# Expert tiles in fours instead of pairs, with single buffers between the steps

## The chip, the cores and the metric

The kernel runs on one core of a Trainium2 chip. The metric is the time of one execution on the device in microseconds (us), lower is better. The kernel before took 1149.71 us, the median of 3 runs (1145.74 to 1151.64).

## The reference

Two transformer layers over 2048 tokens of width 128. Layer 0 has full attention with 16 heads of 8, layer 1 causal attention with 8 heads of 16. Between them stands the part that the change touches, a mixture of 16 experts of which each token takes one, beside a shared network:

```python
logits = hidden @ router_w.T
top_vals, top_idx = jax.lax.top_k(logits, 1)
scores = sigmoid(top value at its expert, 0 elsewhere)
gate, up = split(einsum('nth,nhf->ntf', hidden * scores, gate_up_proj))
routed_out = einsum('ntf,nfh->nth', up * silu(gate), down_proj)
shared = silu(hidden @ shared_gate_w.T) * (hidden @ shared_up_w.T) @ shared_down_w.T
x = x + gb * (shared + routed_out.sum(axis=0))
```

Layer 1 then normalises x again, projects keys, queries and values, and ends with a token-mixing network of its own.

## The kernel before

The tokens are worked on in four chunks of 512. A planner written in Python (make_plan) puts all the work of the kernel into one list of named stages. Each engine's program walks through this list and emits its own part of each stage, so the order within every engine is that of the list. The backbone is 336 steps of attention (256 for layer 0, 80 for layer 1). A step has two pairs of transposed scores ("st", L846 in layer 0, L855 in layer 1), which ScalarE turns into exponentials (L1351), score tiles for the row maxima ("s", L805 and L812), which VectorE reduces (L1120), and the product of probabilities and values ("pv", L875).

All other work is booked into a step with at(), at_side(). TensorE's stages wait in a book called later, and do_later() takes one of them, that of the earliest step, at each call. There are two calls in a step (three from the last unit of layer 0 on). A second book, after, holds the work of layer 1's mixing network and is served when nothing in the first is due. at_side() is for stages without TensorE, done when their step comes.

A tensor of results in PSUM takes a turn of a bank. There are three single banks T0 to T2, taken in rotation by beside() and by the transposed scores, and two double banks S0 and S1, taken in turn by between() and the score tiles. A turn waits until the engine that empties the bank has freed it.

The tokens of chunks 0 to 2 (group 0, 28 tiles of 128) and of chunk 3 (group 1, 20 tiles) are sorted by expert: GpSimd scatters them to memory, SyncE loads them back (XS). The tiles go through three products, now by pairs:

- m0: two tiles are transposed into one T bank (L951), ScalarE copies them to hS (L1407).
- m1: gate and up products of both tiles into one bank of an S turn (L961). ScalarE takes tanh of the gates into tS (L1413), VectorE multiplies twice (L1237, L1241) into acS and frees the bank.
- m2: the down products into a T bank (L969), ScalarE copies them back to XS (L1417), and SyncE stores every second pair's four tiles (L1699).

hS, tS and acS have two buffers each. The weights of an expert tile are one fetch of 192 KB by SyncE (L1693) into one of 16 slots in group 0 and 8 in group 1; a slot is fetched anew when the m2 of its earlier tile is done on TensorE.

When a group is through, GpSimd gathers the results (L1590), and setup1 prepares a chunk for layer 1 at fixed steps: acceptance and statistics on VectorE (L1247, L1249, L1070, L1074), the turn (L764), the projections k1 and q1 (L776), whose parts VectorE splits (L1092 to L1096), SyncE stores and loads again (L1631, L1653, L1660), and the values (L791), which VectorE copies (L1254). Layer 1 may compute score tiles of a chunk from three steps after its projections on. The shared network runs beside as four "up" stages (L919, L920, with L1401, L1180, L1184) and a "down" (L929, freed by L1189).

Of the kernel before, what the change touches and what calls it, by code (L numbers as in the profile page):

```python
# [13 lines left out]
CH = 512  # L14
# [93 lines left out]
def make_plan():  # L108
# [23 lines left out]
    def at_side(step, *fns):  # L132
        at(step, *fns, book=light)
# [57 lines left out]
    def experts(s, g, pace):  # L191
        n = GROUPS[g][3] // 2

        def first(p):
            if p < n:
                beside("m0", g, p)
            if 0 <= p - 2 < n:
                beside("m2", g, p - 2)
                for k in (2 * p - 4 + SLOTS[g], 2 * p - 3 + SLOTS[g]):
                    if k < GROUPS[g][3]:  # L200
                        P.stage("fetch", g, k)
        for p in range(n + 2):
            at(s + int(pace * p), lambda p=p: first(p))
            if 0 <= p - 1 < n:
                at(s + int(pace * p), lambda p=p: between("m1", g, p - 1))
        return s + int(pace * (n + 1)) + 1
# [6 lines left out]
    def setup1(s, c):  # L213

        def accept():
            P.stage("accept", c)
            P.stage("stats", 2, c)

        def turn():
            P.turn_h(2, c, P.next_t())  # L220
            P.xb += 1
            P.stage("bias1", c)

        def rows():
# [5 lines left out]
            ready[c] = now[0] + 3  # L230

# [19 lines left out]
    def after_chunk(L, c, t):  # L251
# [5 lines left out]
        elif c == 2:  # L257
# [4 lines left out]
            s = experts(s, 0, 1)  # L262
            for i in range(3):
                at_side(s, lambda i=i: P.stage("gather", i))
            shared(s - 1, 1, 1)
            setup1(s + 3, 0)
            setup1(s + 5, 1)
            shared(s + 4, 2, 1)
            setup1(s + 9, 2)
        else:  # L270
# [3 lines left out]
            s = experts(s, 1, 0.6)  # L274
            at_side(s, lambda: P.stage("gather", 3))
            setup1(s + 3, 3)
# [221 lines left out]
def adaln_two_layers(nc, A, out):  # L498
# [3 lines left out]
    with ctx:  # L502
# [100 lines left out]
        hS, tS, acS = ([Vf[:, 6656 + 512 * k + 256 * i:6656 + 512 * k + 256 * i + 256] for i in range(2)] for k in range(3))  # L603
# [95 lines left out]
        def gates_ups(bank):  # L699

            v = bank.rearrange("p (k two n) -> p k two n", k=2, two=2)
            return v[:, :, 0, :], v[:, :, 1, :]

        def two_before(g, p):

            return (g, p - 2) if p >= 2 else (0, GROUPS[0][3] // 2 - 2 + p) if g else None
# [1053 lines left out]
```

## Time and profile before

| | |
|---|---|
| median of 3 runs | 1149.71 us |
| profiled execution, its own time | 1151.61 us |
| its span, first to last instruction | 1149.2 us |
| TensorE busy | 1021.7 us, 89% |
| VectorE busy | 903.9 us, 79% |
| ScalarE busy | 814.9 us, 71% |
| GpSimd busy | 149.0 us, 13% |
| mean granted clock of TensorE | 0.949 |

Busy time is the share of the span in which an engine executes instructions. An engine that is busy for most of a stretch sets its length; where none is, the waits between them do. So the table by stretch and the waits within a stretch tell more than the whole. The granted clock is the share of full TensorE speed, where 1 stands for 2.4 GHz and 0.5 for 1.2 GHz. Expert products of group 0 run from about 645 to 713 us, those of group 1 from about 890 to 943 us.

### The profile page before, as it was taken

The numbers are of one execution on the slowest core, as the hardware profiler recorded it, in microseconds if no ns is written. First come the engines' busy times: TensorE is split into PE (matmuls) and PEld (weight loads), VectorE is DVE, ScalarE is ACT, GpSimd is POOL, SyncE is SP. The second block draws the span as 40 slices with busy tenths as digits, with TensorE's granted clock in tenths as the row PEclk, the third lists the DMA queues.
The fourth block names the chain that finished last, engine by engine and source line by source line (L and its number), as shares of the span: only waits on it lengthen the run. The fifth ranks groups of instructions, "written<-read, shape, count | busy, mean of one in ns | idle before, by whom it ended". The sixth has DMA issues, their size and how long they took to land.

```text
span 1149.2 us, 22131 instructions
## 1 busy us (share of the span) xinstructions
PE 1021.7 (89%) x8766; PEld 349.2 (30%) x8766; DVE 903.9 (79%) x1154; ACT 814.9 (71%) x1556; POOL 149.0 (13%) x264
## 2 busy tenths in 40 slices
PE   4658999999999999999998999899978888798895
PEld 1212222222222222222232444343434443233323
DVE  5897999998999989999988777666766568587602
ACT  3105999998999998999976676567743555466683
POOL 2005000004000013000034000410121003000100
PEclk8658999999999999999999999999989999899997
DMA  4650400002000001000003431052003211200000
GB/s 105 128 98 17 137 2 2 2 2 44 1 2 2 2 21 23 2 1 3 2 2 116 122 87 31 27 93 49 1 1 111 74 57 28 38 10 2 10 1 9
DMA packets 47259, 42.04 MB, mean 37 GB/s; under 512 B 6102, under 2 KB 45366, under 8 KB 47158
## 3 DMA queue, kind: packets, MB, share of 16 engines
q1 hardware_dynamic: 44902, 35.27, 13.2%
q0 software_dynamic: 1824, 5.25, 1.6%
q8 instruction: 70, 1.15, 0.4%
q14 instruction: 31, 0.25, 0.1%
q10 hardware_dynamic: 432, 0.13, 0.0%
HBM read 26.83 MB, written 13.30 MB: 35 GB/s over the span
## 4 chain that ended last, share of the span: by engine, by line
PE 65%; DVE 21%; ACT 7%; issue 3%; DMA 2%; POOL 1%; SPq 1%; POOLq 0%; DVEq 0%; ACTq 0%
PE O L875 23%; DVE mx L1120 13%; PE T L846 12%; PE S L805 7%; PE S L812 4%; ACT PT L1351 3%; PE T L855 3%; PE S L961 2%; PE S L919 1%; PE S L929 1%; PE T L969 1%; PE S L920 1%; PE S L855 1%; PE T L884 1%; DVE Vf L1180 1%
## 5 line engine op out<-in xcount | busy, mean ns | idle before, releaser
L1120 DVE TENSOR_REDUCE mx<-S 128x2 f32<-128x1024 f32 (+2 forms) x672 | 757.0, 1179 | 89.2 <-PE S L812 38.2
L1351 ACT ACTIVATE PT<-T 128x512 f32<-128x512 f32 (+2 forms) x1280 | 675.8, 581 | 118.1 <-PE T L846 46.8
L875 PE MATMUL O<-PT,Va 128*9 128x256 f32 (+1 forms) x4040 | 319.0, 388 | 3.3 <-ACT Os L1358 3.3
L805 PE MATMUL S<-Ks,Qs 48*128 48x512 bf16 x1024 | 208.0, 397 | 26.3 <-DVE mx L1120 22.0
L846 PE MATMUL T<-Qs,Ks 51*128 51x512 bf16 x1024 | 202.1, 387 | 15.3 <-ACT PT L1351 7.2
L846 PEld LDWEIGHTS T<-Qs,Ks 51*128 51x128 bf16 x1024 | 55.6, 93 | 226.4 <-issue 131.9
L875 PEld LDWEIGHTS O<-PT,Va 128*9 128x9 f32 x4040 | 60.0, 88 | 207.4 <-issue 198.0
L812 PE MATMUL S<-K,Qs 96*128 96x512 bf16 (+3 forms) x320 | 85.5, 358 | 15.7 <-DMA Qs<-rows_q 5.4
L855 PE MATMUL T<-Qs,K 99*128 99x512 bf16 (+3 forms) x256 | 72.2, 350 | 7.7 <-ACT PT L1351 4.0
L875 PE MATMUL O<-PT,V 128*17 128x512 f32 (+3 forms) x640 | 75.0, 541 | 0.0
L805 PEld LDWEIGHTS S<-Ks,Qs 48*128 48x128 bf16 x1024 | 52.5, 95 | 53.4 <-DVE mx L1120 47.9
L1530 POOL CAST n<-nm 128x16 bf16<-128x16 f32 x24 | 5.6, 233 | 411.8 <-DVE nm L1128 411.6
L1336 ACT ACTIVATE nrow<-T 12x512 bf16<-12x512 bf16 x24 | 14.1, 586 | 47.2 <-PE T L825 47.1
L812 PEld LDWEIGHTS S<-K,Qs 96*128 96x128 bf16 x320 | 29.2, 99 | 53.1 <-issue 13.7
L855 PEld LDWEIGHTS T<-Qs,K 99*128 99x128 bf16 x256 | 22.7, 99 | 45.3 <-issue 33.3
L1139 DVE RECIPROCAL rl<-T 128x16 f32<-128x16 f32 x8 | 2.0, 254 | 42.8 <-PE T L884 42.8
L1180 DVE SCALAR_TENSOR_TENSOR Vf<-Vf,S 128x512 f32<-128x512 f32 x16 | 11.0, 687 | 30.6 <-ACT Vf L1401 30.5
L1345 ACT ACTIVATE PT<-S 128x1024 f32<-128x1024 f32 (+3 forms) x32 | 28.5, 941 | 7.0 <-PE S L855 5.6
L1237 DVE SCALAR_TENSOR_TENSOR Vf<-Vf,S 128x256 f32<-128x256 f32 x24 | 10.1, 421 | 28.2 <-ACT Vf L1413 28.2
L1401 ACT ACTIVATE Vf<-S 128x512 f32<-128x512 f32 x16 | 9.6, 597 | 31.1 <-PE S L920 31.1
L1309 ACT ACTIVATE hT<-T,mc 128x512 f32<-128x512 f32 x16 | 12.5, 779 | 26.4 <-PE T L764 26.1
L1545 POOL TENSOR_TENSOR vw<-om,rl 128x128 f32<-128x128 f32 x16 | 6.5, 407 | 185.6 <-DVE rl L1134 185.6
(225 smaller groups left out, 835.3 us busy)
## 6 DMA issues: line engine op xcount, KB each, us to landing
Qs<-in_L_ffn_experts SPq DMA_DIRECT2D x28, 192.0 KB, 2.7
Ks<-in_L_ffn_experts SPq DMA_DIRECT2D x20, 192.0 KB, 2.6
Qs<-rows_q SPq DMA_DIRECT2D x48, 64.0 KB
Vf<-sorted_x SPq DMA_DIRECT2D x12, 256.0 KB, 4.5
sorted_y<-Vf SPq DMA_DIRECT2D x12, 256.0 KB, 2.3
Qs<-rows_q SPq DMA_DIRECT2D x24, 128.0 KB, 4.6
rows_q<-q SPq DMA_DIRECT2D x7, 384.0 KB, 2.6
sorted_x<-XP POOLq DMA_DIRECT2D x1, 1792.0 KB, 10.8
```

Of the source, the lines that this page charges most:

```text
L805: m = e.matmul(two[:, i, :], Qs[r0:r0 + 48, hp, q0:q0 + 128], Ks[r0:r0 + 48, hp, CH * kb:CH * kb + CH], start=True, stop=True, tile_positi ...
L812: m = e.matmul(two[:, i, 0:n], Q1[0:96, 4 * quad + 2 * pair + i, q0:q0 + 128], K1[0:96, CH * kb:CH * kb + n], start=True, stop=True)
L846: m = e.matmul(bank, Ks[r0:r0 + 51, hp, keys], Qs[r0:r0 + 51, hp, CH * c:CH * c + CH], start=True, stop=True, tile_position=(r0, 0))
L855: m = e.matmul(bank[:, lo:CH], K1[0:99, keys], Q1[0:99, 4 * quad + 2 * pair + i, CH * c + lo:CH * c + CH], start=True, stop=True)
L875: m = e.matmul(Ob[32 * g:32 * g + d1, lo:hi], v, PT[(2 * j + g // 2) % 4][:, p0 + lo:p0 + hi], start=(kt == 0 and halves[0] == 0), stop=Tr ...
L961: m = e.matmul(bank[:, 256 * k + 128 * h:256 * k + 128 * h + 128], w_of(g, i)[:, 128 * h:128 * h + 128], hS[p % 2][:, 128 * k:128 * k + 12 ...
L1120: e.tensor_reduce(mx[:, u % 2, h0:h0 + 2, kb], two[:, :, 0:n], AX.X, ALU.max).then_inc(free, 1)
L1180: dv.tick(e.scalar_tensor_tensor(bt, bsg, 1.0, two[:, 0, :], ALU.add, ALU.mult))
L1309: e.activation(hc(c), bank, ACT.Identity, bias=mc[:, layer, k:k + 1], scale=mc[:, layer, k + 1:k + 2]).then_inc(free, 1)
L1336: e.activation(nrow[:, U % 2, :], bank.bitcast(BF16)[0:12, 0:CH], ACT.Copy).then_inc(free, 1)
L1345: e.activation(both, Sb[turn["st", L, j, 2 * pair][0]][:, :, lo:CH], ACT.Exp).then_inc(free, 1)
L1351: e.activation(PT[(2 * j + pair) % 4][:, CH * i + lo:CH * i + CH], bank[:, lo:CH], ACT.Exp).then_inc(free, 1)
```

## The change

Tiles go through the three products by fours. m0 fills a whole T bank with four turned tiles. m1 takes both banks of an S turn, four gates in the first and four ups in the second, so that tanh and the multiplications are of 512 columns. m2 fills a whole T bank with four results, and each m2 is followed by its store and the fetches into its four slots. hS, tS and acS have one buffer of 512 columns each in the same memory. The planner books m1 of a four and m0 of the next into one step, and m2 into the step after; fours are 2 steps apart in group 0 and 1.2 in group 1.

What comes after the experts is no longer booked at fixed steps: the last m2 calls then(), which books gathers and setup1, and each part of setup1 books the next when it has been staged. Acceptance is put off while the shared "down" of its chunk is not yet planned.

```diff
+    def experts(s, g, pace, then):
+        n = GROUPS[g][3] // 4
+        def last(q):
+            beside("m2", g, q)
+            for k in range(4 * q + SLOTS[g], min(4 * q + 4 + SLOTS[g], GROUPS[g][3])):
+                P.stage("fetch", g, k)
+            if q == n - 1:
+                then(now[0] + 1)
+        at(s, lambda: beside("m0", g, 0))
+        for q in range(n):
+            t = s + 1 + int(pace * q)
+            at(t, lambda q=q: between("m1", g, q))
+            if q + 1 < n:
+                at(t, lambda q=q: beside("m0", g, q + 1))
+            at(t + 1, lambda q=q: last(q))
+        return s + 1 + int(pace * (n - 1)) + 2
...
         def accept():
+            if ("down", c) not in P.turn:
+                at_side(now[0] + 1, accept)
+                return
             P.stage("accept", c)
             P.stage("stats", 2, c)
+            at_side(now[0] + 1, lambda: P.norm(2, c))
+            at(now[0] + 2, turn)
...
-        at_side(s + 1, lambda: P.norm(2, c))
-        at(s + 2, turn)
-        at(s + 3, rows)
-        at(s + 4, values)
...
-            s = experts(s, 0, 1)
+            def rows1(s):
+                for i in range(3):
+                    at_side(s, lambda i=i: P.stage("gather", i))
+                setup1(s + 3, 0)
+                setup1(s + 5, 1)
+                shared(s + 4, 2, 1)
+                setup1(s + 9, 2)
+            s = experts(s, 0, 2, rows1)
...
-            s = experts(s, 1, 0.6)
+            experts(s, 1, 1.2, rows1)
...
-        hS, tS, acS = ([Vf[:, 6656 + 512 * k + 256 * i:6656 + 512 * k + 256 * i + 256] for i in range(2)] for k in range(3))
+        hS, tS, acS = (Vf[:, 6656 + CH * k:6656 + CH * k + CH] for k in range(3))
...
+                    two = Sb[turn["m1", g, q][0]]
+                    done(("m0", g, q))
+                    for k in range(4):
+                        i = 4 * q + k
                         pe.wait_ge(w_fetched[g][i % SLOTS[g]], 16 * (i // SLOTS[g] + 1))
                         for h in range(2):
+                            m = e.matmul(two[:, h, 128 * k:128 * k + 128], w_of(g, i)[:, 128 * h:128 * h + 128], hS[:, 128 * k:128 * k + 128],
+                                         start=True, stop=True)
...
-                    e.activation(two_tiles(tS[p % 2]), gates_ups(bank)[0], ACT.Tanh, scale=0.5).then_inc(expert_sig, 1)
+                    e.activation(tS, bank, ACT.Tanh, scale=0.5).then_inc(expert_sig, 1)
```

## Rows read from the trace of the kernel before

**Rows 1.** Busy time by stretch (us from the span's start)

```profile
core 0: us, PE busy (x) PEld busy (x) DVE busy (x) ACT busy (x) POOL busy (x), PEclk, DMA share, GB/s
644.50:713.75 69.25, 66.65 (x605) 32.15 (x601) 51.17 (x64) 51.52 (x112) 1.27 (x5) 1.00 0.21 59
...
889.80:943.40 53.60, 43.58 (x320) 26.15 (x319) 30.86 (x44) 26.72 (x66) 0.87 (x4) 1.00 0.22 64
943.40:969.30 25.90, 23.29 (x149) 10.62 (x146) 22.75 (x38) 15.54 (x29) 8.01 (x11) 1.00 0.08 22
```

**Rows 2.** Waits of TensorE, 890 to 945 us: total, times, longest

```profile
PE T L969 <- DVE Vf L1241: 3.8, 6, 1.0
PE S L961 <- DVE mx L1120: 2.3, 3, 0.9
PE S L812 <- DVE Vf L1241: 1.7, 3, 0.7
```

**Rows 3.** Timeline of TensorE in group 0: start, length, instruction

```profile
672.54 1.16 PE L961 MATMUL S<-Vf,Qs 128*128 128x128 f32 x8
673.63 0.39 PE L846 MATMUL T<-Qs,Ks 51*128 51x512 bf16 x2
673.85 0.38 PE L805 MATMUL S<-Ks,Qs 48*128 48x512 bf16 x2
...
674.71 0.44 PE L951 MATMUL T<-idf,Vf 128*128 128x128 f32 x2
675.24 0.68 PE L969 MATMUL T<-Qs,Vf 128*128 128x128 f32 x4
675.86 0.39 PE L846 MATMUL T<-Qs,Ks 51*128 51x512 bf16 x2
...
687.94 0.66 PE L884 MATMUL T<-idf,Os 128*128 128x128 f32 x4
688.52 0.39 PE L846 MATMUL T<-Qs,Ks 51*128 51x512 bf16 x2
```

**Rows 4.** Groups of instructions by shape: count, busy us, mean ns, idle before

```profile
L1120 DVE TENSOR_REDUCE mx<-S 128x2 f32<-128x1024 f32 x624 | 725.3, 1217 | 74.8 <-PE S L812 38.2 <-PE S L805 26.2 <-PE S L815 8.3
...
L1180 DVE SCALAR_TENSOR_TENSOR Vf<-Vf,S 128x512 f32<-128x512 f32 x16 | 11.0, 687 | 30.6 <-ACT Vf L1401 30.5
...
L1237 DVE SCALAR_TENSOR_TENSOR Vf<-Vf,S 128x256 f32<-128x256 f32 x24 | 10.1, 421 | 28.2 <-ACT Vf L1413 28.2
...
L1401 ACT ACTIVATE Vf<-S 128x512 f32<-128x512 f32 x16 | 9.6, 597 | 31.1 <-PE S L920 31.1
...
L1413 ACT ACTIVATE Vf<-S 128x256 f32<-128x256 f32 x24 | 9.2, 383 | 24.0 <-PE S L961 23.9
```

**Rows 5.** Timeline of TensorE, single places; idle time and its end in brackets

```profile
754.00 0.65 PE L764 MATMUL T<-idf,XP 128*128 128x128 f32 x4 [1.20 <-DVE V L1254]
...
902.89 1.16 PE L961 MATMUL S<-Vf,Ks 128*128 128x128 f32 x8
...
905.51 0.60 PE L812 MATMUL S<-K,Qs 96*128 96x512 bf16 x2 [0.59 <-DVE Vf L1241]
...
969.29 1.02 PE L776 MATMUL T<-hT,wk 128*16 128x512 f32 x2
...
987.24 1.87 PE L812 MATMUL S<-K,Qs 96*128 96x512 bf16 x4 [5.40 <-DMA Qs<-rows_q]
```

**Rows 6.** Timeline of VectorE: acceptance of chunk 1, split of chunk 3

```profile
742.69 0.68 DVE L1247 TENSOR_TENSOR XP<-XP,gB 128x512 f32<-128x512 f32 x1
...
745.04 0.38 DVE L1074 BATCH_NORM_AGGREGATE mv<-st 128x2 f32<-128x6 f32 x4
...
971.63 0.68 DVE L1092 TENSOR_TENSOR qf<-qf,q 16x512 f32<-16x512 f32 x1 [1.19 <-ACT q L1325]
...
974.57 0.69 DVE L1096 TENSOR_TENSOR q<-qf,q 128x512 bf16<-128x512 f32 x1
```

**Rows 7.** Timeline of SyncE's queue: two fetches of group 1

```profile
897.13 1.13 SPq L1693 DMA_DIRECT2D Ks<-in_L_ffn_experts  x2
```

**Rows 8.** The page's DMA issues: fetches of group 1, us to landing

```profile
Ks<-in_L_ffn_experts SPq DMA_DIRECT2D x20, 192.0 KB, 2.6
```

More of the change, by code:

```diff
@@ L189, in sort @@
         return s + 2
[L191 to L206, printed above, removed]
+    def experts(s, g, pace, then):
[14 more added lines that the diff above has]
+        return s + 1 + int(pace * (n - 1)) + 2
     def shared(s, c, apart):
@@ L222, in turn @@
             P.stage("bias1", c)
+            at(now[0] + 1, rows)
         def rows():
@@ L230, in rows @@
             ready[c] = now[0] + 3
+            at(now[0] + 1, values)
         def values():
@@ L273, in after_chunk, with rows1 @@
             shared(t + 6, 3, 1)
-            s = experts(s, 1, 0.6)
-            at_side(s, lambda: P.stage("gather", 3))
-            setup1(s + 3, 3)
+            def rows1(s):
+                at_side(s, lambda: P.stage("gather", 3))
+                setup1(s + 3, 3)
+            experts(s, 1, 1.2, rows1)
     P.stage("silu")
@@ L697, in w_of, with four_before @@
             return Wt[g][k % SLOTS[g]]
[L699 to L706, printed above, removed]
-        def two_tiles(v):
-            return v.rearrange("p (k n) -> p k n", k=2)
+        def four_before(g, q):
+            return (g, q - 1) if q else (0, GROUPS[0][3] // 4 - 1) if g else None
         def pe_program(e):
@@ L946, in pe_program @@
                 elif name == "m0":
-                    g, p = a
-                    bank, full = opened(("m0", g, p))
-                    pe.wait_ge(x_sorted[g][p // 2], 16)
-                    for k in range(2):
-                        m = e.transpose(bank[:, 128 * k:128 * k + 128], XS[:, 2 * p + k, :], idf[:, :])
+                    g, q = a
+                    bank, full = opened(("m0", g, q))
+                    pe.wait_ge(x_sorted[g][q], 16)
+                    for k in range(4):
+                        m = e.transpose(bank[:, 128 * k:128 * k + 128], XS[:, 4 * q + k, :], idf[:, :])
@@ L952, in pe_program @@
                     m.then_inc(full, 1)
                 elif name == "m1":
-                    g, p = a
-                    bank, full = opened(("m1", g, p))
-                    done(("m0", g, p))
-                    for k in range(2):
-                        i = 2 * p + k
+                    g, q = a
+                    _, full = opened(("m1", g, q))
+                    two = Sb[turn["m1", g, q][0]]
+                    done(("m0", g, q))
+                    for k in range(4):
+                        i = 4 * q + k
@@ L963, in pe_program @@
                     m.then_inc(full, 1)
                 elif name == "m2":
-                    g, p = a
-                    bank, full = opened(("m2", g, p))
-                    done(("m1", g, p))
-                    for k in range(2):
-                        m = e.matmul(bank[:, 128 * k:128 * k + 128], acS[p % 2][:, 128 * k:128 * k + 128], w_of(g, 2 * p + k)[:, 256:384],
-                                     start=True, stop=True)
+                    g, q = a
+                    bank, full = opened(("m2", g, q))
@@ L971, in pe_program @@
+                    done(("m1", g, q))
+                    for k in range(4):
+                        m = e.matmul(bank[:, 128 * k:128 * k + 128], acS[:, 128 * k:128 * k + 128], w_of(g, 4 * q + k)[:, 256:384], start=True, stop=True)
                     m.then_inc(full, 1)
```

61 lines of the change are left out of this document (25 added, 36 removed).

## Prediction

> **What bounds the kernel now.** I read the table of busy time by stretch first. In the first expert stage (group 0, 644.5 to 713.75 us) TensorE is busy 66.65 of 69.25 us, VectorE 51.17 and ScalarE 51.52 [rows 1]. So every instruction that TensorE issues there costs, and the other two have cover. In the second (group 1, 889.8 to 943.4) TensorE is busy 43.58 of 53.6 us, and no other engine more than 30.86 [rows 1]: here waits set the pace. Behind it (943.4 to 969.3) VectorE is busy 22.75 of 25.9 us [rows 1].
>
> The chain of waits of group 1 names them: products m2 that wait for VectorE's activation (3.8 us, 6 times), products m1 that wait for a score reduction to empty their bank (2.3 us, 3 times), and score tiles that wait until m1's bank is empty (1.7 us, 3 times) [rows 2]. Together 7.8 us; smaller ones bring the idle time of the stretch to 10.0 us.
>
> **The change, part by part.**
>
> *TensorE's work.* Products and transposes are the same in number; only the turns halve, 72 to 36. In the timeline of group 0 the eight records of m1 take 1.09 us to the next instruction, the four of m2 0.62 [rows 3]. The slope is 0.1175 us a record, so 0.15 us of each turn is fixed; joining two saves 0.15 for m1 and for m2. Two transposes take 0.53 us to the next instruction, four (those of the attention result) 0.58 [rows 3]: joining saves 0.48. Per four tiles 0.78 us; seven fours in group 0 give 5.5 us. In group 1 I take 0.6 each, since fixed parts there lie partly under waits: 3.0 us.
>
> *The chain through ScalarE and VectorE.* It becomes longer for each turn. Half-width instructions took 383 ns (tanh), 421 and about 421; full-width ones of the same kind 597, 687 and about 687 [rows 4]. The bank of m1 comes free at 905.51 behind an m1 of 902.89 [rows 5]; less its 1.09 that is 1.5 us, of which 1.2 are the three instructions and 0.3 hand-over. After the change it is 2.0 + 0.3 = 2.3 us. ScalarE and VectorE save some 36 fixed parts of 0.17 us and a few of 0.15; both have cover, so I count nothing for it.
>
> *New stall, group 0.* Each step of layer 0 has two score tiles, and there are two banks. Now m1 and the next tile of its bank are far enough apart. After the change the plan puts m1 ahead of the first pair of transposed scores, and the next m0 in the second slot. Between m1 and the second score tile, on m1's bank, lie: first half of the step 1.08 us [rows 3], m0 of four 0.58, the second pair 0.22 (673.63 to 673.85). That is 1.88 us against 2.3: a stall of 0.4, six times, and 0.95 at the last four, which has no m0 to fill it. ScalarE's queue is tighter too (a 0.6 us copy and tanh ahead of the exponentials): 0.15 more for each four. New stalls 0.4 x 6 + 0.95 + 0.15 x 7 = 4.4 us. They take most of the 5.5. Gain in group 0: about 1 us (bounds: 5.5 if the stalls stay hidden, -3 if ScalarE's delays double them).
>
> *Group 1.* Pace 1.2 and three slots a step: m1 comes behind the two score tiles, so each of four m1 waits about 0.9 for the reduction of its bank (a reduction takes 1217 ns [rows 4]; the products of the other tile, 0.60 us by their record [rows 5], of which I count 0.43 before the next can start, cover part, and hand-over adds 0.1). The first m1 has its bank's next tile 0.86 behind it: 1.4 us. Three m2 follow at 1.9 us a chain of 2.3: 0.4 each. Sum 1.4 + 3.6 + 1.2 = 6.2, against 10.0 idle now: 3.8 gained, of which I leave 0.8 for waits that I don't see. With the 3.0 of turns it is 6.0 us. The planner's queue also empties sooner: the last m2 is staged at step 279, not 280; the mixing turn of chunk 0 moves from 281 to 278 and its products from 283 and 285 to 280 and 282. That work is not lost, but leaves the stretch where VectorE is nearly full [rows 1], which is why I let the 6.0 us pass through. Bounds 2 and 9.
>
> *Setup of layer 1.* setup1 now chains itself. By hand through the planner's queues: gathers at step 232 (before 233), acceptance of chunk 0 at 235 (236), but its projections k1, q1 at 240 (239), since the shared products of chunk 2 hold slots ahead of it. In step 240 come projections of chunk 0, the shared result of 32 records (at the slope above 3.8 us), and projections of chunk 1; before, the two chunks' projections were two steps apart. Scores of layer 1 start at 243 (242). Queued on VectorE behind one another are then: split of chunk 0, result of chunk 2, split of chunk 1, acceptance and statistics of chunk 2, and only then the copy of chunk 0's values, which frees the T bank that the values of chunk 1 want (they are three T turns apart). Prices: the split begins 2.3 us after the projection (969.29 to 971.63) and both parts take 3.6 (to 975.26); acceptance with statistics takes 2.7 us (742.69 to 745.42) [rows 5, 6]. From the first projection: the second ones start at 2.0 + 0.3 + 3.8 + 0.3 = 6.4 (two projections, a pair of transposed scores, the shared result, a pair), their split at 8.7, its end at 12.3, acceptance 15.0, copy 15.2. TensorE comes to chunk 1's values at 6.4 + 2.0 + 1.0 + 1.0 + 0.3 = 10.7 (projections, probabilities, chunk 0's values, a pair; eight records of the slope are 1.0). A stall of some 4.5 us; the kernel now pays 1.20 us at the like place (754.00 [rows 5]). Net loss 3.3, with other small waits 3.5 us (bounds 0, if the copy comes earlier than I think, and 6). It covers the loads of q1, which need 18 us from projection to landing (969.29 to 987.24 [rows 5]): TensorE would be at the first score after about 21.
>
> *Unchanged.* The wait of 5.40 us for q1 of chunk 3 at 987.24 [rows 5]: gather, acceptance and projection stay at steps 280, 283, 286, scores at 289. The loads start from the projection, so the wait moves with it, whole. Stores stay 12, fetches 48. Group 1 has only eight weight slots: the four fetches behind one m2 must land before the next m1 but one, about 9.2 us later. One takes 2.6 us to land [rows 8], they leave SP some 0.8 us apart (two starts within 1.13 less 0.33 [rows 7]), and the copy and the store ahead of them take about 1.7: first landed after 4.7, fourth after 7.1, and it is wanted 1.5 later than the first. Hidden, with 3 us to spare.
>
> **Sum.** -1 - 6 + 3.5 = -3.5 us. The profiled execution has a span of 1149.2 and its own time is 1151.61, the median 1149.71: the gain carries over as it is, since all of it lies inside. Forecast 1149.7 - 3.5 = 1146.2, rounded to 1146.
>
> **A rule against the change.** The rows show what grows: m1's bank is held 0.8 us longer a turn [rows 4]. The Trainium skill, page "Perfetto Trace Analysis", section "Optimizing Scalar/DVE Operations", says that where ScalarE and VectorE are not saturated but cause bubbles on other engines, breaking instructions up may let work complete sooner; this change does the reverse. By it the time would be that of the third rival below; the trace agrees in part, for bubbles exist in group 1 and hardly in group 0.
>
> **Rivals.**
> - *No new stall in setup.* The values' copy is in time; the rest as above. 1149.7 - 7.0 = 1142.7. For it: now 1.20 us suffices; against it: the queue worked out above. Chance 0.24.
> - *The gain is taken back.* Group 1 gains only its turns (3.0), group 0 nothing, setup loses as said: 1150. Chance 0.14.
> - *Long chains bind in both stages.* Each four pays at its bank (2.3 less 1.1) and at m2 (0.6): 1.8 us a four, 21.6 for twelve, against 8.5 of turns and 7.8 of present waits saved; with setup 21.6 - 16.3 + 3.5 = 8.8 slower, 1158.5. It decides from (16.3 - 3.5) / 12 = 1.07 us a four on. For it: single buffers and two banks; against it: m0 lies between m1 and the bank's next use. Chance 0.11.
> - *Weights late in group 1.* If SP stands behind ScalarE's copies 3 us longer, three m1 wait 3 us each: +9 - 3.5, 1155. The slack of 3 us would have to go. Chance 0.05.
> - *The forecast* 0.46, own range 1142.5 to 1149.5.
>
> **Numbers.** A change of 0.5% (5.75 us) is about what a measurement of this kernel can tell from none: below 1144.0 is faster, above 1155.5 slower. Faster: the first rival, less a little, and a quarter of the forecast's own range, 0.34. Slower: most of the third and a part of the weights, 0.13. Same 0.53. The range 1140 to 1156 leaves out the upper half of the chains' rival and the case in which no new stall comes and group 1 gains its full 9.
>
> **What would show it.** Group 0: idle time of TensorE for VectorE at a score tile of 0.4 us, once each four, and m1 of 16 records in about 2.05 us to the next instruction. Group 1: its expert products over some 4 to 6 us sooner after their start, m2's waits at most three. Setup: one wait of TensorE of 3 to 5 us for VectorE's copy of the values, ahead of the second products of values, around 40 us behind the last expert product of group 0. If that wait is absent the first rival holds; if the wait of 5.40 has changed by more than 1 us, my reading of the q1 chain is wrong. A granted clock that falls behind the new stall, as at 987.24, where four score products took 1.87 us, would cost up to 1.5 us more.

## The result and the profile after

| | before | after |
|---|---|---|
| median of 16 runs each | 1149.85 us | 1155.39 us |
| lowest and highest | 1145.37 to 1153.24 | 1151.67 to 1157.06 |
| profiled execution, own time | 1151.61 us | 1152.05 us |
| its span | 1149.2 us | 1150.0 us |

The changed kernel is slower: ratio 1.0049, 95% interval 1.0036 to 1.0061, some 5.6 us. The profiled execution of before was one of its slow ones and that of after one of its fast ones, so these two profiles differ by 0.4 us only. They show where the kernel changed, not the whole of the loss.

The busy time by stretch, the same stretches as before [rows 1]:

```profile
core 0: us, PE busy (x) PEld busy (x) DVE busy (x) ACT busy (x) POOL busy (x), PEclk, DMA share, GB/s
644.50:713.75 69.25, 65.63 (x584) 32.82 (x576) 47.61 (x49) 45.45 (x88) 4.63 (x9) 1.00 0.22 65
889.80:943.40 53.60, 46.12 (x342) 27.82 (x340) 31.53 (x37) 28.24 (x59) 3.46 (x7) 1.00 0.25 71
943.40:969.30 25.90, 22.70 (x130) 9.61 (x130) 22.16 (x38) 12.25 (x23) 6.60 (x9) 0.93 0.06 17
```

TensorE works 46.12 us in the second stretch where it worked 43.58. The waits there, from 890 to 945 us (total, times, longest), stand against [rows 2]:

```profile
PE S L963 <- DVE mx L1121: 3.4, 4, 0.9
PE S L813 <- DVE Vf L1241: 1.3, 1, 1.3
PE T L971 <- DVE Vf L1241: 1.2, 3, 0.4
PE S L813 <- DVE mx L1121: 1.1, 3, 0.5
PE T L885 <- ACT Vf L1407: 0.3, 1, 0.3
PE T L971 <- ACT nrow L1336: 0.2, 1, 0.2
```

In the changed file m0 is L952, m1 L963, m2 L971, a transposed score pair L847 in layer 0, a score tile L806 in layer 0 and L813 in layer 1. Group 0 in TensorE's timeline, against [rows 3]:

```profile
665.09 2.05 PE L963 MATMUL S<-Vf,Qs 128*128 128x128 f32 x16
667.07 0.39 PE L847 MATMUL T<-Qs,Ks 51*128 51x512 bf16 x2
...
668.16 0.66 PE L952 MATMUL T<-idf,Vf 128*128 128x128 f32 x4
668.90 0.39 PE L847 MATMUL T<-Qs,Ks 51*128 51x512 bf16 x2
669.34 0.39 PE L806 MATMUL S<-Ks,Qs 48*128 48x512 bf16 x2
...
672.64 0.39 PE L847 MATMUL T<-Qs,Ks 51*128 51x512 bf16 x2 [0.18 <-ACT PT L1351]
673.73 2.05 PE L963 MATMUL S<-Vf,Qs 128*128 128x128 f32 x16
...
704.24 0.39 PE L806 MATMUL S<-Ks,Qs 48*128 48x512 bf16 x2 [0.64 <-DVE Vf L1241]
```

One m1 of four takes 1.98 us to the next instruction (665.09 to 667.07), two of before took 2.18. The idle times in brackets are small: 0.18 for a probability tile once a four, and 0.64 at the last four. From one m1 to the next (665.09 to 673.73) a four takes 8.64 us, where two pairs took 8.81.

The setup of layer 1, in TensorE's timeline:

```profile
757.81 0.59 PE L777 MATMUL T<-hT,wk 128*16 128x512 f32 x1
758.33 1.13 PE L777 MATMUL T<-hT,wq 128*128 128x512 f32 x2
759.39 1.04 PE L876 MATMUL O<-PT,Va 128*9 128x512 f32 x8
760.36 1.06 PE L792 MATMUL T<-wv,hT 128*128 128x16 f32 x8
761.36 0.39 PE L847 MATMUL T<-Qs,Ks 51*128 51x512 bf16 x2
766.45 1.89 PE L792 MATMUL T<-wv,hT 128*128 128x16 f32 x8 [4.70 <-DVE V L1254]
768.27 0.61 PE L847 MATMUL T<-Qs,Ks 51*128 51x512 bf16 x2
```

This is the forecast stall: the second products of values wait 4.70 us for VectorE's copy of the first, where the kernel before waited 1.20 us for such a copy at 754.00 [rows 5]. What VectorE does in that time:

```profile
760.00 0.68 DVE L1093 TENSOR_TENSOR qf<-qf,q 16x512 f32<-16x512 f32 x1 [2.17 <-ACT q L1325]
...
762.95 0.69 DVE L1097 TENSOR_TENSOR q<-qf,q 128x512 bf16<-128x512 f32 x1
763.55 0.69 DVE L1247 TENSOR_TENSOR XP<-XP,gB 128x512 f32<-128x512 f32 x1
...
765.90 0.38 DVE L1075 BATCH_NORM_AGGREGATE mv<-st 128x2 f32<-128x6 f32 x4
766.20 0.19 DVE L1254 COPY V<-T 128x64 f32<-128x64 f32 x1
```

The split of chunk 1, then the acceptance and statistics of chunk 2, then the copy of 0.19 us for which TensorE stands. From 1 us into the wait on, the granted clock is at its lower level, 1.2 GHz, for most of 14 us:

```profile
757.00:763.00 6.00, 4.75 (x26) 1.69 (x24) 3.54 (x7) 4.98 (x9) 0.00 (x0) 0.98 0.44 130
763.00:777.00 14.00, 9.78 (x44) 4.11 (x44) 4.79 (x18) 3.97 (x8) 2.05 (x4) 0.52 0.80 131
```

So the waits that the prediction named in group 1 and in the setup are there; of the 0.4 us that it expected at a score tile in each four of group 0, only that of the last four is. What it did not foresee is that the sum has the other sign.

### The profile page after: what moved, and what is told of

It is laid out like the page before. It is cut to its first block, busy times and chain, and to the rows that moved or that the text cites. A ratio compares the mean times of both kernels' runs of the same rounds, so it can differ in the third digit from the quotient of the medians.

```text
span 1150.0 us, 21977 instructions
## 1 busy us (share of the span) xinstructions
PE 1021.5 (89%) x8758; PEld 351.4 (31%) x8758; DVE 900.5 (78%) x1130; ACT 807.6 (70%) x1520; POOL 148.9 (13%) x264
## 4 chain that ended last, share of the span: by engine, by line
PE 65%; DVE 20%; ACT 7%; issue 3%; DMA 2%; POOL 1%; SPq 1%; POOLq 0%; DVEq 0%; ACTq 0%
PE O L876 23%; DVE mx L1121 12%; PE T L847 12%; PE S L806 7%; PE S L813 4%; ACT PT L1351 3%; PE T L856 3%; PE S L963 2%; PE S L920 1%; PE S L921 1%; PE T L885 1%; PE T L971 1%; PE S L856 1%; PE S L930 1%; ACT PT L1345 1%
## 5 line engine op out<-in xcount | busy, mean ns | idle before, releaser
L876 PE MATMUL O<-PT,Va 128*9 128x256 f32 (+1 forms) x4032 | 319.8, 389 | 3.3 <-ACT Os L1358 3.3
L806 PE MATMUL S<-Ks,Qs 48*128 48x512 bf16 x1024 | 208.2, 398 | 28.6 <-DVE mx L1121 22.7
L847 PE MATMUL T<-Qs,Ks 51*128 51x512 bf16 x1024 | 203.1, 389 | 17.3 <-ACT PT L1351 10.2
L847 PEld LDWEIGHTS T<-Qs,Ks 51*128 51x128 bf16 x1024 | 55.9, 93 | 231.7 <-issue 131.2
L876 PEld LDWEIGHTS O<-PT,Va 128*9 128x9 f32 x4032 | 60.0, 89 | 204.2 <-issue 194.9
L813 PE MATMUL S<-K,Qs 96*128 96x512 bf16 (+3 forms) x320 | 86.0, 360 | 16.8 <-DVE mx L1121 6.3
L876 PE MATMUL O<-PT,V 128*17 128x512 f32 (+3 forms) x640 | 75.2, 543 | 0.0
L806 PEld LDWEIGHTS S<-Ks,Qs 48*128 48x128 bf16 x1024 | 52.7, 96 | 58.9 <-DVE mx L1121 48.3
L813 PEld LDWEIGHTS S<-K,Qs 96*128 96x128 bf16 x320 | 29.7, 99 | 54.9 <-issue 14.1
L816 PE MATMUL S<-mq,idb 128*128 128x128 bf16 x128 | 26.1, 223 | 0.0
```

Of the source, the lines that this page charges most:

```text
L806: m = e.matmul(two[:, i, :], Qs[r0:r0 + 48, hp, q0:q0 + 128], Ks[r0:r0 + 48, hp, CH * kb:CH * kb + CH], start=True, stop=True, tile_positi ...
L813: m = e.matmul(two[:, i, 0:n], Q1[0:96, 4 * quad + 2 * pair + i, q0:q0 + 128], K1[0:96, CH * kb:CH * kb + n], start=True, stop=True)
L816: m = e.matmul(two[:, i, n - 128:n], idb[:, :], mq[:, :], start=False, stop=True, skip_group_check=True)
L847: m = e.matmul(bank, Ks[r0:r0 + 51, hp, keys], Qs[r0:r0 + 51, hp, CH * c:CH * c + CH], start=True, stop=True, tile_position=(r0, 0))
L876: m = e.matmul(Ob[32 * g:32 * g + d1, lo:hi], v, PT[(2 * j + g // 2) % 4][:, p0 + lo:p0 + hi], start=(kt == 0 and halves[0] == 0), stop=Tr ...
```

## The experiments

Times are compared with runs of the kernel before on the same chip (its medians there 1158.1 to 1158.6 us). To tell where time went I measured, in each profile, the time between the same steps of the plan, each from the start of its first product of probabilities and values (L876 here). With it goes the time that the granted clock was at its lower level in that stretch, from the clock records of the same trace.

| kernel | setup of layer 1 | waits filled | ratio to before | 95% interval |
|---|---|---|---|---|
| changed kernel again | chained | no | 1.0033 | 1.0007 to 1.0059 |
| fours, fixed setup | fixed | no | 0.9997 | 0.998 to 1.0013 |
| pairs, chained setup | chained | no | 1.0062 | 1.0033 to 1.009 |
| fours, third chunk later | chained, +1 | no | 1.0022 | 1.0005 to 1.0039 |
| fours, second and third later | chained, +1 +1 | no | 1.0004 | 0.9981 to 1.0027 |
| fours in group 1 only | fixed | no | 1.0007 | 0.9987 to 1.0027 |
| the same, m1 in the third slot | fixed | no | 1.0020 | 1.0001 to 1.0039 |
| changed, one wait filled | chained | values' copy | 1.0040 | 1.0027 to 1.0052 |
| before, waits filled | fixed | the others | 0.9969 | 0.9955 to 0.9983 |
| fours, fixed setup, filled | fixed | the others | 0.9917 | 0.9899 to 0.9934 |
| changed, filled | chained | all | 0.9969 | 0.9956 to 0.9982 |
| changed, values first, filled | chained | the others | 0.9982 | 0.9969 to 0.9996 |
| fours in group 1 only, filled | fixed | the others | 0.9943 | 0.9931 to 0.9956 |
| fours in group 0 only, filled | fixed | the others | 0.9964 | 0.9946 to 0.9982 |

**First: is it the fours or the setup?** Theory setup puts the loss on the chained setup stages, theory chains on the longer single-buffered turns of four. The changed kernel with the setup stages at their fixed steps of before:

```diff
-                then(now[0] + 1)
+                then(now[0] + (1 if g else 2))
...
-            if ("down", c) not in P.turn:
-                at_side(now[0] + 1, accept)
-                return
...
+        at_side(s + 1, lambda: P.norm(2, c))
+        at(s + 2, turn)
+        at(s + 3, rows)
+        at(s + 4, values)
```

> The tiles stay in fours, but each part of the setup for layer 1 is booked at fixed steps again, as in the kernel before (projections of the chunks at steps 239, 241, 245 and scores from 242 on). Theory setup: the loss comes from TensorE's wait of 4.70 us for the copy of the values and from the half clock behind it; it goes away, and the time is about 1149 us, no more than the kernel before. Theory chains: the longer chains of single buffers cost in the expert stages; the time stays at about 1155 us.

Measured 0.9997. The pairs of before with the chained setup stages (the same chaining lines added to the kernel before):

```diff
         def accept():
+            if ("down", c) not in P.turn:
+                at_side(now[0] + 1, accept)
+                return
...
+            at_side(now[0] + 1, lambda: P.norm(2, c))
+            at(now[0] + 2, turn)
...
-        at_side(s + 1, lambda: P.norm(2, c))
-        at(s + 2, turn)
-        at(s + 3, rows)
-        at(s + 4, values)
```

> The kernel before with its pairs, but with the setup for layer 1 that books each of its parts when the one ahead is staged. Here the projections fall on steps 239, 241 and 245, so they do not meet in one step, and the values of chunk 1 come in step 242 behind the acceptance of chunk 2. Theory setup: a wait of 1 to 3 us for the values' copy, 1150 to 1152 us. Theory chains: the setup costs nothing, 1150 us.

Measured 1.0062. This is not the converse of the experiment ahead of it: with pairs the two chunks' projections fall on steps 239 and 241 as before, so chaining only changes the order within steps 240 and 241. And its executions fall into two groups, five at 1159.2 to 1162.2 us and seven at 1169.3 to 1172.1, with the profiled one among the long ones (the median of the kernel before is 1158.24 there). In that profile the wait for the values' copy is 0.7 us only, and steps 236 to 246 took 51.95 us, against 47.07 in the kernel before. The clock was at its lower level for 10.2 us of them, against 3.4, which can be up to 3.4 us of the difference. The rest, and why seven of twelve executions are 10 us longer, is open. That the loss of the changed kernel goes with its setup rests on the first experiment, and more firmly on the same pair of kernels with the waits filled (below): here the two intervals, 0.9997 and 1.0033, still touch.

The changed kernel once more, unchanged, on that chip:

> The changed kernel once more, for a second profile. Both theories: 1155 us; the profile shows how much of the time between the layers is the same in each execution: the wait of 4.7 us is there again, the stretches at half clock may lie elsewhere.

Measured 1.0033, which agrees with 1.0049. And the changed kernel with only the setup of the third chunk a step later, then with those of the second and the third:

```diff
-                setup1(s + 9, 2)
+                setup1(s + 10, 2)
```

> The changed kernel with the acceptance of chunk 2 one step later (242 for 241), so that VectorE copies the values of chunks 0 and 1 ahead of its 2.7 us. Theory setup: the wait of 4.70 us falls to about 2 us, and the half clock behind it may go; 1151 to 1153 us. Theory chains: no change from 1155 us.

Measured 1.0022; the wait for the values' copy is 1.79 us. Steps 236 to 246 took 45.5 us in its profile, less than in the kernel before (47.07), so what this variant still loses lies elsewhere: 1.1 us in steps 246 to 263, since the scores of layer 1 start at step 243 and not 242, and 2.0 in steps 292 to 305, with 6.8 us at the lower clock (below).

```diff
-                setup1(s + 5, 1)
+                setup1(s + 6, 1)
...
-                setup1(s + 9, 2)
+                setup1(s + 10, 2)
```

> The changed kernel with two setup stages of the next layer moved: the second chunk's one step later (its projection lands in the step after that of the first, 240 becomes 239 and 241), the third's one step later; the fours of both groups stay as they are. Theory setup (the 0.5% lies in the values' copy queued behind the splits and the acceptance, TensorE's wait of 4.70 us for it, and the half clock behind the wait): the wait for the first chunk's values' copy is under 2 us, no half-clock stretch of 13.7 us stands at 763 to 777, and the ratio to the kernel before is 0.998 to 1.001. Theory chains (fours with single buffers are what is lost): nothing is given back, ratio 1.003 to 1.006. A third reading, that any later chunk costs because its scores then start later (as the variant with only the third chunk moved gave 1.0022): 1.001 to 1.003.

Measured 1.0004. The wait is gone (1.06 us of products of values without idle time before them), and steps 236 to 246 took 46.51 us where the changed kernel took 49.49 on its second chip. The scores of layer 1 start at step 242 again (51.9 us for steps 246 to 263, not 53.0). By the ratios, the further the two chunks are pulled apart, the less is lost; the intervals of neighbours overlap.

**Second: where is the gain of the fours?** The fixed setup gives back the loss, but leaves no gain, though steps 263 to 292, with group 1, took 161.0 us in the fours with fixed setup and 165.3 in the kernel before. So I tried group 1 alone. The generator of the stage takes four or two tiles by group; the pair functions are those of the kernel before:

```diff
+W = (2, 4)
...
+            s = experts2(s, 0, 1)
```

> Pairs in group 0 as before, fours in group 1 alone, and the setup stages at their steps of before. Theory setup: group 1 alone gives about 2 us (steps 263 to 292 were 4.4 us shorter at their start and 2.4 us longer at their end), so the ratio is 0.996 to 0.999, under that of the fours in both groups with the old setup (0.9997), if group 0's fours cost anything at all in the scatter and gather stretches. Theory chains: group 1's chain of acceptance, gate copy and result waits costs more than the pairs', ratio 1.000 to 1.003.

Measured 1.0007, while its profile has steps 263 to 292 at 158.8 us, 6.5 us below the kernel before. Not all of that is the fours': 2.9 us of it lie ahead of group 1's first turned tiles, where this profile has 3.4 us at the lower clock and that of the kernel before 10.2. From those first turned tiles on the profiles sort by tiles and by clock:

| profile | tiles in group 1 | at the lower clock, us | first m0 of group 1 to step 292, us |
|---|---|---|---|
| before, both chips | pairs | 6.8 | 116.7 and 116.5 |
| before, waits filled | pairs | 3.4 | 116.6 |
| fours in group 0 only, filled | pairs | 0 | 115.0 |
| changed, first profile | fours | 13.7 | 116.7 |
| fours, fixed setup | fours | 10.2 | 115.1 |
| changed again; group 1 only | fours | 6.8 | 112.9 and 112.8 |
| fours, fixed setup, filled | fours | 3.4 | 113.1 |

Group 1's products themselves always gain the same: from the first m0 to the start of the last m2 it is 44.7 us in all eleven profiles with fours at this pace, and 52.7 in four of the five with pairs (54.3 in the pairs with chained setup). Of these 8.0 us, 4.3 are paid back before step 292. Of those, 2.9 are one new wait, of a score tile for a reduction on VectorE, which all eleven have and none of the five. At 6.8 us of lower clock 3.7 us are left. And in seven of the eleven the clock falls during that wait or within 2 us behind it, for 3.4 or 6.8 us, where no profile with pairs has it fall; in the changed kernel's first profile, with 13.7 us at the lower clock, nothing is left. There:

```profile
955.74 0.34 PE L813 MATMUL S<-K,Qs 96*128 96x384 bf16 x1 [2.85 <-DVE mx L1121]
...
958.98 1.91 PE L813 MATMUL S<-K,Qs 96*128 96x512 bf16 x4
```

Four such products take 1.03 us at the full clock (below). The same kernel with m1 a half step later, behind the second pair of transposed scores, and fours one step apart instead of 1.2:

```diff
-            at(t, lambda q=q: between("m1", g, q))
+            if q + 1 < n:
+                third[t] = lambda q=q: between("m1", g, q + 1)
```

> As the kernel with fours in group 1 alone, with the gates and ups of each four put into the step's third slot, a half step later than the turned tiles, so that TensorE has two score tiles between the turn and its copy's reader. If the waits of 0.8 to 0.9 us per four for the turned tiles' copy behind the score acceptance are worth their time, the waits at the gates and ups fall under 0.3 us each and the ratio is 0.994 to 0.998. If the stretch is held by VectorE (25.0 of 29.4 us busy in steps 280 to 286), the waits go and the time does not: 0.998 to 1.000. Theory chains: removing the waits gives back the loss, ratio 0.003 under that of fours in group 1 alone.

Measured 1.0020. The waits of m1 (L1001 here) for reductions are 0.3 us at most, as expected, but others took their place. Waits of TensorE from 890 to 960 us:

```profile
PE S L1001 <- DMA Ks<-in_L_ffn_experts: 5.1, 3, 3.1
PE S L848 <- DVE mx L1160: 1.1, 2, 0.9
PE T L891 <- ACT PT L1395: 0.9, 1, 0.9
PE S L1001 <- DVE mx L1160: 0.6, 2, 0.3
```

The weights are late: with fours one step apart there are fewer steps between a four's fetches and their use. That is the mechanism of the prediction's rival of late weights, and at pace 1.2 it has not come. Slot and pace were changed together, so the later slot by itself was not tried.

The kernel before was profiled on that chip too.

> The kernel before, for a profile on the same chip as the variants. If the stops of TensorE, ScalarE and VectorE during the scatters and gathers (about 4 us in steps 105 to 216 and 7 us in steps 231 to 236 in four profiles of variants) belong to the chip and not to the change, they stand here too.

1159.2 us, span 1157.4. The stops during the gathers stand here as well (ScalarE, then TensorE; see the last section), so they are not the change's.

Timeline of TensorE at the start of score unit 6 of layer 1, where it waits for the rows of shifts; first the kernel before:

```profile
1048.21 0.59 PE L855 MATMUL T<-Qs,K 99*128 99x512 bf16 x2 [2.48 <-DMA Qs<-nrow]
1048.64 1.03 PE L812 MATMUL S<-K,Qs 96*128 96x512 bf16 x4
```

Then the changed kernel, run again:

```profile
1046.87 1.01 PE L856 MATMUL T<-Qs,K 99*128 99x512 bf16 x2 [2.48 <-DMA Qs<-nrow]
1047.68 1.91 PE L813 MATMUL S<-K,Qs 96*128 96x512 bf16 x4
```

The same wait of 2.48 us, and behind it the same four score products take 1.03 us in one and 1.91 in the other. The table of stretches gives the granted clock there (1044 to 1058 us) as 1.00 and 0.76. Whether this wait is followed by the lower clock differed from profile to profile; steps 292 to 305 took 40.8 us with it absent and 42.1 to 43.1 with it present (absent in 5 profiles of the 11 in which the wait is unfilled). The mean granted clock of the timed runs says how much lower clock there is in all: 0.9513 (35 runs) and 0.9530 (29 runs) for the kernel before, and 0.9455 to 0.9496 for the seven variants above. At two levels, the time at the lower one is 2 x (1 - clock) x span: 109 to 113 us in the kernel before, 117 to 126 in the variants, the pairs with chained setup (0.9472) among them.

**Third: take the lower clock away.** TensorE executes added fp32 products with an unused result, in the bank that the next instruction has taken anyway, just ahead of its long waits. The work of the reference is as before.

```diff
+            def warm(bank, n):
+                if n:
+                    pe.wait_ge(po_const, PO["id"])
+                    for _ in range(n):
+                        e.matmul(bank[:, 0:128], idf[:, :], idf[:, :], start=True, stop=True)
...
+                        if c == 3 and rows_loaded["q1", c].name not in pe.met:
+                            warm(two[:, 0, :], 14)
...
+                    warm(bank0, {(0, 15, 1): 14, (1, 6, 0): 8, (1, 7, 0): 8}.get((L, u, kt), 0) if pair == 0 else 0)
```

The entry (0, 15, 1) is the place ahead of the values' copy; 14 more stand ahead of the last turned tile, 8 ahead of group 1's rank, 7 ahead of mix_k of the last chunk. First only the values' copy in the changed kernel:

> The changed kernel with 14 added fp32 products of 128 by 128 (results unused, some 3.4 us in all at the full clock) on TensorE just ahead of the transposed scores that stand before its wait of 4.70 us for the copied values, so that the wait is filled and the clock does not fall, while VectorE's queue is as late as before. Theory clock (the setup's cost is mostly the half clock behind the wait): the granted clock is 1.0 where it was half from 763 to 777, and the ratio is 0.002 to 0.004 under that of the changed kernel (1.0033 and 1.0049). Theory stall (the cost is the wait itself): the wait shrinks to about 1 us, the step ends as late as before, and the ratio stays at 1.003 to 1.005.

```profile
772.21 3.37 PE L727 MATMUL T<-idf 128*128 128x128 f32 x28
...
777.09 1.07 PE L798 MATMUL T<-wv,hT 128*128 128x16 f32 x8 [1.19 <-DVE V L1261]
```

The wait is filled (1.19 us left) and the products behind it run at the full clock (1.07 us, not 1.89), but the ratio is 1.0040, as without. The granted clock tells why this doesn't decide between the two theories:

```profile
765.00:779.00 14.00, 12.81 (x98) 8.85 (x96) 10.39 (x27) 6.64 (x13) 1.26 (x2) 1.00 0.65 127
779.00:786.00 7.00, 6.22 (x31) 1.99 (x24) 0.77 (x4) 3.58 (x8) 0.88 (x2) 0.51 0.63 110
```

The lower clock was put off, from right behind the wait to 2 us later, and not avoided. It shows as well that the wait costs by itself: with the clock full up to 779, steps 238 to 240 took 17.39 us, only some 1.4 less than without the products (18.72 and 18.86).

Then all the waits, in three kernels on the same chip:

> The kernel before with the same products ahead of the same waits, but for the values' copy, which waits for 1.2 us only. Theory clock: half-clock stretches of 6.8 us at the last chunk's queries and at the shift rows go, the ratio is 0.990 to 0.997. Theory stall: 0.999 to 1.002.

> Fours in both groups with the setup stages at their steps of before, and the same products as in the kernel before. If group 1's gain (3 to 6 us in the profiles of steps 263 to 292) is what the half clock behind the later waits gives back, this is the fastest kernel: 0.003 to 0.006 under the kernel before with the same products. If the fours by themselves are worth nothing, the two are equal within 0.002.

> The changed kernel with such products ahead of all of TensorE's long waits from step 240 on: the values' copy (4.70 us), the one-hot table (2.72), the last chunk's queries (4.70 to 5.40), the shift rows (2.48 and 2.71), the last normalised tile (4.69) and the last mixed tile (2.41). Theory clock (all variants of fours have 4 to 14 us more of half clock by their mean granted clocks than the kernel before, 0.946 to 0.950 against 0.951 to 0.953): the stretches at half clock go, the mean clock rises by 0.01 or more, and the ratio falls to 0.990 to 0.998. Theory stall: half-clock stretches hide behind other engines, ratio 1.002 to 1.005.

The fours with the fixed setup, TensorE ahead of the last chunk's queries and ahead of the shift rows:

```profile
982.85 3.34 PE L724 MATMUL S<-idf 128*128 128x128 f32 x28
987.82 1.04 PE L819 MATMUL S<-K,Qs 96*128 96x512 bf16 x4 [1.63 <-DMA Qs<-rows_q]
...
1038.60 2.05 PE L724 MATMUL T<-idf 128*128 128x128 f32 x16
1041.07 0.60 PE L863 MATMUL T<-Qs,K 99*128 99x512 bf16 x2 [0.41 <-DMA Qs<-nrow]
```

And the first of these places with the wait not filled:

```profile
990.34 1.87 PE L810 MATMUL S<-K,Qs 96*128 96x512 bf16 x4 [4.74 <-DMA Qs<-rows_q]
```

With the waits filled, the kernel before is at 0.9969, the changed kernel at 0.9969, and the fours with fixed setup at 0.9917, the fastest kernel of all (1149.0 us against 1158.59 on that chip). The mean granted clocks are 0.9617, 0.9617 and 0.9628, which is 88, 88 and 85 us at the lower level. Two differences of one chip follow. The fours are worth 0.0052, 6.0 us, once the clock stays up, and the chained setup costs 0.0052, 6.0 us, each to within some 2.5 us by the intervals (the fastest kernel has six executions only); in the profiles, for the setup, steps 236 to 246 take 49.6 us against 45.6 and steps 246 to 263 take 53.0 against 51.9, together 5.1. Of these at most 3.5 us can be the 7 us at the lower clock (779 to 786 above; in the changed kernel with all waits filled 778 to 785), so the rest, 1.6 us or more, is waits and order.

From 0.9997 to 0.9917 the filling was worth 0.0080, 9.3 us, for some 31 us less at the lower clock, measured on two chips. In the kernel before, on one chip, it was worth 3.6 us for 21. The Trainium skill, page "TensorE: Matmul & The Clock Gate", section "Terms", puts the penalty at half the throttled time; an estimate by it would be 16 us for the first and 10 for the second. Much of the lower-clock time lies where TensorE waits or another engine sets the pace, so the measured price is the one to use.

**Fourth: is it the copy's place in the queue?** The same changed kernel with filled waits, with the first chunk's values projected and copied ahead of that chunk's own splits:

```diff
             project("q1", c, P.next_t())
+            if c == 0:
+                values()
             split("k1", c, "dv")
...
-            at(now[0] + 1, values)
+            if c:
+                at(now[0] + 1, values)
```

> The changed kernel with one thing moved: the first chunk's values are projected and copied ahead of that chunk's own splits, in step 240, instead of in step 241 behind both chunks' splits and the acceptance of chunk 2; no other step moves. The waits other than the values' copy are filled with unused products as in the kernel before with filled waits (0.9969) and in the changed kernel with filled waits (0.9969). Theory queue (the changed setup costs 0.5% because the values' copy is queued behind the splits and the acceptance on VectorE): the wait of 4.70 us is gone and the ratio is 0.991 to 0.994, that of the fours with the setup steps of before (0.9917). Theory crowding (both chunks' projections, splits and the acceptance in two steps cost the same wherever the copy stands): the wait comes back at another instruction, 0.996 to 0.998.

TensorE, and then VectorE's copy:

```profile
772.33 1.07 PE L802 MATMUL T<-wv,hT 128*128 128x16 f32 x8
...
778.14 0.61 PE L860 MATMUL T<-Qs,Ks 51*128 51x512 bf16 x2 [4.41 <-DVE V L1269]
```

```profile
772.40 0.42 DVE L1110 CAST q<-qf 16x512 bf16<-16x512 f32 x1
...
775.24 0.68 DVE L1262 TENSOR_TENSOR XP<-XP,gB 128x512 f32<-128x512 f32 x1
...
777.89 0.19 DVE L1269 COPY V<-T 128x64 f32<-128x64 f32 x1
```

The first wait is gone and a wait of 4.41 us stands at the next T turn, for the copy of the second chunk, queued behind its own splits and the same acceptance. The ratio is 0.9982, not the 0.991 to 0.994 of theory queue. So it isn't where one copy stands. Two chunks' splits and an acceptance follow one another on VectorE, whose last two pieces alone fill 760.00 to 766.20 in the changed kernel, and whichever T bank waits behind them is late.

**Fifth: which group gains?** Fours in one group alone, fixed setup, waits filled:

> Pairs in group 0 and fours in group 1 alone, the setup steps of before, the other long waits filled. If group 1 is what the fours gain (3.5 us in steps 263 to 292 of the profiles with filled waits), the ratio is 0.003 under the kernel before with filled waits: 0.993 to 0.995. If group 0 brings it: 0.996 to 0.998.

> Fours in group 0 and pairs in group 1, the setup steps of before, the other long waits filled. If group 0's fours neither gain nor cost (steps 216 to 236 took 95.25 and 95.11 us in two profiles, 238 to 246 some 1.6 us less): 0.995 to 0.997. If the two gains add up to that of both groups (0.9917 against 0.9969), this and the kernel with fours in group 1 alone lie 0.005 in sum under the kernel before with filled waits.

0.9943 (five executions) and 0.9964 against 0.9969 for pairs in both. Group 1 is worth 0.0026, 3.0 us; group 0 0.0005, 0.6 us, with intervals of 0.0012 to 0.0018 to either side in each ratio, and from different chips. Together they make 0.0031 against 0.0052 for both at once, a difference within those intervals.

## Why the prediction was wrong

The forecast was 1149.7 - 1 - 6 + 3.5 = 1146.2. Step by step:

- *Turns.* Right for m1; the turned tiles are under the next point. m1 of four takes 1.98 us to the next instruction where 2.05 was expected and two took 2.18 before.
- *New stall, group 0.* Near in the net, and partly by luck. Forecast was a gain of 1 us, 5.5 less 4.4. A four takes 8.64 us where two pairs took 8.81: 0.17 each, 1.2 for seven. But both terms were too large. Four transposes take 0.74 us to the next instruction (668.16 to 668.90) and not 0.58, so a four's turns save some 0.67 us and not 0.78; and the 0.4 us of waiting at a score tile stands at no four but the last (0.64 for 0.95). In its place are 0.18 at a probability tile and some 0.2 between the pair behind the turned tiles and its score tile (668.90 to 669.34, against 0.22 elsewhere). Steps 216 to 236 took 95.25 us before and 95.11 after, and the experiment gives 0.6.
- *Group 1.* The waits came as written: 1.33 for 1.4 at the first bank, four of 0.77 to 0.89 for 0.9, three of 0.31 to 0.44 for 0.4. In all TensorE waits 7.5 us from 890 to 945 against 6.2 forecast. The group's products were over 8.0 us sooner, where 4 to 6 was forecast. The rule of the Trainium skill, page "Perfetto Trace Analysis", section "Optimizing Scalar/DVE Operations", on breaking instructions up was set against the change; here the trace goes the other way, since with tanh and multiplications of double width the group was shorter.
- *The step that failed first:* "which is why I let the 6.0 us pass through". Of the 8.0 us by which group 1 ends sooner, 3.7 are left at step 292 at the same time at the lower clock; by the ratios, group 1 alone gives 3.0 us with the clock kept up, and next to nothing arrives without: 1.0007 alone, 0.9997 with both groups. In the stretch behind group 1 a new wait of 2.85 us stands at 955.74 (a score tile for a reduction, VectorE busy 22.16 of 25.9 us), the clock falls at it in seven of eleven profiles, and the variants run 4 to 18 us longer at the lower clock in all. The prediction read the clock only behind its own stall ("up to 1.5 us more") and never as something that takes a gain elsewhere.
- *Setup, the other step that failed, by its size.* The mechanism was named rightly, with its step, its queue and its wait (4.5 forecast, 4.70 measured). Mis-sized was the term: 3.5 us, where the difference of kernels measured 4.2 us (1.0033 less 0.9997) and 6.0 with filled waits. The wait was priced, but not that the scores of layer 1 start a step later (1.1 us in steps 246 to 263), nor the second chunk's own copy. The wait starts some 55 us behind the last expert product, later than the 40 that were forecast. Half clock was there as said (763 to 777), and 1.5 us was too little for it: of the 14 us at a mean of 0.52 some 3.5 lie inside the wait, and the rest can cost up to 5. How much of the loss it is was not separated, since filling the wait only moved it.
- *Unchanged.* Right. The wait for q1 was 4.70 us at 984.94 against 5.40, within the microsecond allowed; no product waited for weights.

The rivals: "no new stall" fell with the wait of 4.70. "Weights late" came nearest in time, at 1155, by luck: no product waited for weights. "Long chains bind in both stages", at 1158.5, fell too, since the fours by themselves lost nothing. "The gain is taken back" (1150, chance 0.14) was nearest in mechanism; it left the setup at 3.5 and missed that the clock takes the gain. With the measured terms the sum is 1149.7 - 0.3 + 4.2 = 1153.6 (0.9997 is 0.3 us), and 1155.4 was measured; the rest is within the two intervals.

Left open: why the pairs with chained setup lose 0.0062 with a short wait only; how the setup's loss divides between wait and lower clock; and what decides whether a given wait is followed by the lower clock. One added place is known, the wait of 2.85 us behind group 1. The other waits are the same, and yet all seven variants have a lower mean granted clock than the kernel before, the one with pairs too.

## What to carry to other kernels

When a change both speeds up a stage and rebooks what comes after it, undo the rebooking alone before judging the stage: here, with the clock kept up, the one was worth some 6 us and the other cost as much. Compare stretches of two profiles only at the same time at the lower clock: of 6.5 us that one stretch seemed to gain, 3.7 were the change's. A gain read from waits in one stretch must be followed to the end of the kernel, through the stretch where another engine is full and through every long wait of TensorE behind it. And a few unused products in TensorE's unavoidable waits, in a bank that it holds anyway, gave 0.3% to the kernel before and, measured on two chips, 0.8% to the variant with fours.

## What the runs showed of the hardware

Waits of TensorE as short as 2.48 us were followed by the lower clock in some profiles and not in others. A full clock through the wait was no guarantee either: at the values' copy it fell 2 us behind it. The lower clock then lasted 3.4 or 6.8 us; in the tail of the kernel, around a wait of 4.69 us, it lasted 10.2 or 13.7 us where the wait was not filled, and in the profiles of before and after it fell 1 us ahead of that wait. With 28 records of small products in 3.3 us ahead of the wait for the queries, the stretch from 985 to 998 us has a granted clock of 1.00 in the fours with fixed setup, against 0.74 without. Even there the clock fell at 999 for 3.4 us, and in the kernel before with filled waits it fell right behind the wait, at 994 for 3.4 us. The first line is with the waits filled, the second without:

```profile
985.00:998.00 13.00, 9.20 (x72) 4.52 (x71) 8.76 (x10) 4.96 (x13) 0.00 (x0) 1.00 0.10 12
```

```profile
985.00:998.00 13.00, 8.26 (x38) 3.24 (x34) 3.82 (x4) 2.95 (x7) 0.00 (x0) 0.74 0.31 36
```

On the other chips the kernel before took 1158 us where it took 1150 on the first. Its profile there shows two places that the first chip's does not have: steps 105 to 216, with the scatters, are 4 us longer, and steps 231 to 236, with the twelve gathers on GpSimd, 5 us. In the gathers ScalarE, VectorE and TensorE stop together; ScalarE's and then TensorE's first instruction behind it in the kernel before:

```profile
736.28 0.60 ACT L1401 ACTIVATE Vf<-S 128x512 f32<-128x512 f32 x1 [5.58 <-remote]
```

```profile
738.31 0.61 PE L846 MATMUL T<-Qs,Ks 51*128 51x512 bf16 x2 [3.92 <-ACT PT L1351]
```

The trace names no releaser on the core for the stop of ScalarE; that the gathers cause it was not tried.
